# Two-layer graph attention with experts: tile 13 counted for layer 2 alone

## What is computed

```python
def _gat(x, src, dst, W, a_src, a_dst, b, heads, ch, concat):
    h = (x @ W).reshape(n, heads, ch)
    es = (h * a_src).sum(-1)
    ed = (h * a_dst).sum(-1)
    e = leaky_relu(es[src] + ed[dst], SLOPE)
    w = jnp.exp(e - segment_max(e, dst)[dst])
    alpha = w / segment_sum(w, dst)[dst]
    out = segment_sum(h[src] * alpha[:, :, None], dst)
    return (concat or mean over heads) + b

h = relu(layernorm(_gat(x, ..., 4 heads)))
x = x + _gat(h, ..., 1 head)
x = x + experts(layernorm(x))   # top 2 of 8, 256 -> 1024 -> 256, gelu
```

## Time and profile before

| what | us |
|---|---|
| median of three runs | 1459.78 |
| lowest, highest | 1451.67, 1463.59 |
| run that was profiled | 1464.53 |
| its span, first to last instruction | 1462.6 |
| PE busy | 1248.2 |
| DVE busy | 866.2 |
| ACT busy | 670.4 |
| POOL busy | 775.4 |

### The profile page before, as it was taken

One profiled execution on the slowest core, in us unless ns is written; L12 is line 12 of the kernel. 1 busy time (PEld: TensorE's weight loads), 2 busy tenths in 40 slices (PEclk: granted clock), 3 DMA queues, 4 the chain that ended last, 5 costly groups with the idle time before them and its releaser, 6 DMA issues.

```text
span 1462.6 us, 21659 instructions
## 1 busy us (share of the span) xinstructions
PE 1248.2 (85%) x6282; PEld 957.9 (65%) x6283; DVE 866.2 (59%) x2590; ACT 670.4 (46%) x1758; POOL 775.4 (53%) x682
## 2 busy tenths in 40 slices
PE   2667799989999999767798897884599999999997
PEld 1446455545555655355686676773599999999996
DVE  7679798788799877634565774766722222222221
ACT  0348676656667777532243232331033334334432
POOL 4500578676767771056666665740444445444444
PEclk9779899999999999967899998986699999999999
DMA  7002743643553481233464554433033332323221
GB/s 239 5 18 87 198 118 100 177 119 101 163 140 105 139 231 31 102 117 97 149 192 129 180 170 123 139 100 107 8 86 89 99 95 43 91 39 92 38 36 26
DMA packets 138724, 157.86 MB, mean 108 GB/s; under 512 B 60020, under 2 KB 117729, under 8 KB 138649
## 3 DMA queue, kind: packets, MB, share of 16 engines
q0 software_dynamic: 35488, 75.68, 21.1%
q1 hardware_dynamic: 101056, 79.93, 17.7%
q10 hardware_dynamic: 2104, 1.38, 0.4%
HBM read 123.00 MB, written 34.70 MB: 108 GB/s over the span
## 4 chain that ended last, share of the span: by engine, by line
PE 59%; DVE 20%; issue 9%; DMA 4%; ACT 3%; another core or an unknown queue 3%; ACTq 1%; POOL 1%; DVEq 0%; POOLq 0%; SPq 0%
PE bank L1285 12%; PE bank L1403 11%; PE bank L1411 11%; PE bank L1236 9%; PE bank L1357 7%; DVE ring_a L1896 3%; DVE ohk L1618 2%; DMA out_x<-ring_a,si 2%; PE bank L1268 2%; DVE ohs L1614 1%; PE bank L1144 1%; PE bank L1169 1%; ACT ring_a L1017 1%; DVE st L1499 1%
## 5 line engine op out<-in xcount | busy, mean ns | idle before, releaser
L772 POOL DMA_INDIRECT arena<-rows,idx_e x385 | 430.0, 1117 | 254.6 <-issue 91.8
L1285 PE MATMUL bank<-ring_a,slots 128*65 128x384 f32 (+1 forms) x1000 | 333.2, 458 | 35.9 <-DVE ring_a L1896 31.0
L1017 ACT ACTIVATE ring_a<-vbb,slots 128x384 f32<-128x384 f32 (+1 forms) x500 | 243.8, 562 | 14.7 <-DMA vbb<-v_rows 10.9
L1285 PEld LDWEIGHTS bank<-ring_a,slots 128*65 128x65 f32 x1000 | 131.4, 143 | 154.5 <-issue 99.3
L1896 DVE SCALAR_TENSOR_TENSOR ring_a<-ring_a,arena 128x1536 f32<-128x1536 f32 (+1 forms) x125 | 192.1, 1538 | 20.0 <-ACT ring_a L1017 13.4
L1114 ACT ACTIVATE ring_a<-bank,cols 128x128 f32<-128x128 f32 x432 | 128.9, 371 | 160.5 <-PE bank L1403 160.2
L1357 PE MATMUL bank<-h2t,ring_a 128*128 128x257 f32 x650 | 179.3, 416 | 24.6 <-issue 14.1
L1236 PE MATMUL bank<-arena,ring_a 128*128 128x257 f32 (+1 forms) x770 | 193.6, 400 | 5.0 <-issue 3.8
L1236 PEld LDWEIGHTS bank<-arena,ring_a 128*128 128x128 f32 x770 | 154.3, 202 | 42.6 <-issue 12.3
L1357 PEld LDWEIGHTS bank<-h2t,ring_a 128*128 128x128 f32 x650 | 129.2, 208 | 49.1 <-issue 20.7
L823 POOL DMA_INDIRECT gs<-gates,gk x54 | 51.4, 953 | 149.1 <-DVE gk L2046 143.4
(11 more groups left out here) (297 smaller groups left out, 1678.6 us busy)
## 6 DMA issues: line engine op xcount, KB each, us to landing
counts_all<-arena SPq DMA_DIRECT2D x13, 800.0 KB
arena<-counts_all SPq DMA_DIRECT2D x13, 800.0 KB
arena<-in_L_ffn_W SPq DMA_DIRECT2D x8, 1024.0 KB, 7.5
vbb<-v_pairs SPq DMA_DIRECT2D x23, 320.0 KB
arena<-rows,idx_e POOLq DMA_INDIRECT x385
XB<-general_sums SPq DMA_DIRECT2D x38, 130.0 KB
vbb<-in_L_ffn_W SPq DMA_DIRECT2D x4, 1024.0 KB
spare<-in_L_ffn_W SPq DMA_DIRECT2D x4, 1024.0 KB
```

The source lines that it names most:

```text
L772: pool.indirect_dma_start(to[:, k, 0:width], None, table, bass.IndirectOffsetOnAxis(idx_e[:, m * PAIR + k:m * PAIR + k + 1], 0)).then_inc( ...
L1017: ins = act.activation(S1[q % SLOTS1][:, h * k * P:(h + 1) * k * P].rearrange("p (t n) -> p t n", n=P), vb1[:, 0:k, h, :], ACT.Copy, scale ...
L1285: pe.matmul(bank[h][0:CH + 1, 0:w_], slots[:, s, h * (CH + 1):(h + 1) * (CH + 1)], S1[q % SLOTS1][:, h * w_:(h + 1) * w_], start=(s == 0), ...
```

## The change

Tile 13 stays an edge tile in layer 1 and becomes a dense tile in layer 2.

- `NE = 13` is now the number of dense tiles of layer 1, `ND = 14` that of layer 2. Layer 1 keeps its five blocks and 46 pairs. A sixth block of counts, `CB[5] = (13, 1)`, is made beside the steps of layer 1's last block (24 visits at steps 100 to 107) and is stored, but not used in layer 1.
- Layer 2 has seven blocks of two tiles: the last is tiles 12 and 13. Its 42 pairs (`PAIRS2`) are spread over steps 3 to 163 by `3 + p * 164 // 42`; they were 46 over steps 3 to 159. The edge tiles of layer 2 are 14 to 24. Plan steps run to 197, they ran to 191.
- SP stores the counts of tile 13 at step 126. Both first loads of layer 2's counts move to step 127, behind the waits for all stores and for the end of layer 1; the load at step 103 and the wait at step 125 are gone. POOL waits for all stores of counts before it gathers for layer 2.
- The key tables have 112 columns of windows, they had 104. `edge_row` names the row buffer of an edge tile of layer 1; its value is the one before.

The diff, cut to its core:

```diff
-ND = 13
-DW = ND * PER_TILE
-B1 = ((0, 1),) + tuple((t, min(3, ND - t)) for t in range(1, ND, 3))
+NE, ND = 13, 14
+EW, DW = NE * PER_TILE, ND * PER_TILE
+CB = ((0, 1),) + tuple((t, min(3, ND - t)) for t in range(1, ND, 3))
+B1 = CB[:1 + NE // 3]
 B2 = tuple((t, min(2, ND - t)) for t in range(0, ND, 2))
...
-PAIRS = (NW - DW) // 2
+PAIRS, PAIRS2 = (NW - EW) // 2, (NW - DW) // 2
+SKIP = PAIRS - PAIRS2
...
-for _b in range(1, len(B1)):
+for _b in range(1, len(CB)):
     for _n, (_w, _v) in enumerate(visits_of(_b)):
...
-    return min((t - ND + 1) * PER_TILE // 2, PAIRS) - 1
+    return min((t - NE + 1) * PER_TILE // 2, PAIRS) - 1
+
+
+def last_pair2(t):
+    return last_pair(t) - SKIP
...
-PAIR2 = [3 + p * 160 // PAIRS for p in range(PAIRS)]
+PAIR2 = [3 + p * 164 // PAIRS2 for p in range(PAIRS2)]
...
-    groups += [Group([t], False, PAIR2[last_pair(t)] + 2) for t in EDGE_TILES]
+    groups += [Group([t], False, PAIR2[last_pair2(t)] + 2) for t in EDGE_TILES]
...
+        def pair_of(n):
+
+            return n if n < PAIRS else n - PAIRS + SKIP
...
-                if q % NT == 1 and 0 < q // NT < len(B1):
+                if q % NT == 1 and 0 < q // NT < len(CB):
                     store_counts(q // NT)
...
-                if q == (len(B1) - 1) * NT + 3:
+                if q == Q1 + 2:
                     for par in range(2):
-                        sp.wait_ge(s_cst[par], 16 * sum(B1[b][1] for b in range(par, len(B1), 2)))
-                    sp.wait_ge(s_a, (len(B1) - 1) * NT)
+                        sp.wait_ge(s_cst[par], 16 * sum(CB[b][1] for b in range(par, len(CB), 2)))
+                    sp.wait_ge(s_a, Q1)
                     load_counts(0)
-                if q == Q1:
-                    sp.wait_ge(s_a, Q1)
                     load_counts(1)
                     sp.dma_start(fw1[0], f_w1[0].rearrange("(k p) n -> p k n", p=P)).then_inc(s_fw[0], 16)
...
             pool.memset(ring_a[:, W2_AT:W2_AT + P // PW * W_PAIR], 0.0).then_inc(s_wz, 1)
+            for par in range(2):
+                pool.wait_ge(s_cst[par], 16 * sum(CB[b][1] for b in range(par, len(CB), 2)))
             pool.wait_ge(s_ht, 16 * NT)
...
-            for n in range(PAIRS + ROW_SLOTS[1], 2 * PAIRS):
+            for n in range(PAIRS + ROW_SLOTS[1], PAIRS + PAIRS2):
                 gather_rows(n, rows2, T2W)
...
             while q < END1:
+                for w, v, u in VISITS_AT.get(q - 2, ()):
+                    if v == VISITS - 1:
+                        window_out(w)
                 for p in PAIR1_AT.get(q - 2, ()):
                     pair_out(p)
...
-                    after(act, s_on, ND + e - 1)
+                    after(act, s_on, NE + e - 1)
...
-                        act.wait_ge(s_pv, (PAIRS + last_pair(t) + 1) * PAIR)
+                        act.wait_ge(s_pv, (PAIRS + last_pair2(t) + 1) * PAIR)
```

More of the change, by code:

```diff
@@ L82 @@
 assert max(GROUP_N) <= P and DW * VISITS <= 512 and PAIR * P <= (PAD_ROWS - ROWS) * P
-assert LOOP_ROWS <= ND and (NW - DW) % 2 == 0
+assert LOOP_ROWS <= NE and (NW - EW) % 2 == 0 and B1[-1][0] + B1[-1][1] == NE
 assert MAX_TILES + NT + 1 <= SLOT_TILES
@@ L140, in plan1 @@
     groups = [Group(range(t0, t0 + k), True, NT * (b + 1)) for b, (t0, k) in enumerate(B1)]
-    for t in range(ND, NT, 2):
+    for t in range(NE, NT, 2):
         tl = range(t, min(t + 2, NT))
@@ L183, with edge_row @@
 G1, G2 = plan1(), plan2()
+def edge_row(t):
+    return 3 + (t - NE) % 2
+for _t in range(NE, NT - 2):
+    _g, _h = (next(g for g in G1 if t in g.tiles) for t in (_t, _t + 2))
+    assert _g.turn[_g.tiles.index(_t)] - 1 < _h.norm[_h.tiles.index(_t + 2)]
+for _b in range(len(B1) - 1):
+    _g, _h = (next(g for g in G1 if B1[b][0] in g.tiles) for b in (_b, _b + 1))
+    assert max(_g.turn) - 1 < min(_h.norm)
 ORDER1 = [t for g in G1 for t in g.tiles]
@@ L587, in slot_of @@
             return GL2[k], s_g[k], 16 * PAIR * (before + (n - PAIRS) // ROW_SLOTS[1] + 1)
+        def pair_of(n):
+            return n if n < PAIRS else n - PAIRS + SKIP
         def block_of(t):
-            return next(b for b, (t0, k) in enumerate(B1) if t0 <= t < t0 + k)
+            return next(b for b, (t0, k) in enumerate(CB) if t0 <= t < t0 + k)
         def tiles1(b):
-            return range(B1[b][0], B1[b][0] + B1[b][1])
+            return range(CB[b][0], CB[b][0] + CB[b][1])
         def bank_of(use):
@@ L678, in _ @@
                     else:
-                        after(sp, s_oe, t - ND - 1)
+                        after(sp, s_oe, t - NE - 1)
                         sp.dma_start(XE[:, i, 1, :], gen[t * P:(t + 1) * P, :]).then_inc(s_ge1[i], 16)
@@ L703, in _ @@
                     rows = slice(0, P if t < NT - 1 else LAST)
-                    after(sp, s_on, ND + e - 1)
+                    after(sp, s_on, NE + e - 1)
                     sp.dma_start(XB[:, e % 2, 1, :], gen[t * P:(t + 1) * P, :]).then_inc(s_gl2[e % 2], 16)
@@ L767, in gather_rows @@
                 to, s_in, _ = slot_of(n)
-                m = n % PAIRS
-                before = n - ROW_SLOTS[n // PAIRS] if m >= ROW_SLOTS[n // PAIRS] else -1
+                m = pair_of(n)
+                before = n - ROW_SLOTS[n >= PAIRS] if (n if n < PAIRS else n - PAIRS) >= ROW_SLOTS[n >= PAIRS] else -1
                 for k in range(PAIR):
@@ L869, in window_out @@
                 act.wait_ge(s_vis, (w + 1) * VISITS)
-                if b >= 2 and w == B1[b][0] * PER_TILE:
+                if b >= 2 and w == CB[b][0] * PER_TILE:
                     act.wait_ge(s_a, (b - 1) * NT)
-                    act.wait_ge(s_cst[b % 2], 16 * sum(B1[a][1] for a in range(b % 2, b - 1, 2)))
-                i, wi = t - B1[b][0], w % PER_TILE
+                    act.wait_ge(s_cst[b % 2], 16 * sum(CB[a][1] for a in range(b % 2, b - 1, 2)))
+                i, wi = t - CB[b][0], w % PER_TILE
                 act.activation(C1[b][:, :, i * P + wi * WIN:i * P + (wi + 1) * WIN],
@@ L1120, in _ @@
             pe.wait_ge(s_F, 1)
-            for g, (first, step) in enumerate(((0, 1), (DW, 2))):
+            for g, (first, step) in enumerate(((0, 1), (EW, 2))):
                 n = GROUP_N[g]
@@ L1792, in hits @@
             def hits(n, first):
-                p = n % PAIRS
+                p = pair_of(n)
                 after(v, s_pw, n)
```

30 lines of the change are left out of this document (15 added, 15 removed).

## The result

The changed kernel takes 1449.26 us (median of 20 runs, 1441.62 to 1457.54), the kernel before 1460.13 on the same chip (20 runs): ratio 0.9933, 95% interval 0.9916 to 0.9949. It is 0.7% faster, 10.9 us by the medians; the forecast was 7.3 us, or 0.5%, slower.

The account below looks back on a forecast made before the run. TensorE's work and waits were taken to set the time nearly everywhere. 7.0 - 2.3 - 14.5 + 12.9 + 4.2 = +7.3 us on 1459.8 gave 1467 us; its own range was 1458 to 1475, with rivals 1448 to 1479.

Parts of the forecast that it names:

- Layer 2, steps 0 to 149: Layer 2 before its last 25 steps: five pairs fewer at 2.7 us each and about 1.0 of finishing moved out, -14.5 us.
- Rival C: Layer 2: pairs set the pace at 7.7 us each through late slots and gathers, dense steps hidden; 1438 us, chance 0.11.
- The upper bound, 7.7 a pair: Upper case for layer 2, steps 0 to 149: the pair sets the pace, 332.0 us for 43 pairs, 38.6 us gained.
- The last 25 steps: Layer 2, steps 150 to 174: second tile 12.8 us, less 2.6 of idle time filled, plus one pair 2.7; +12.9 us.
- Costs of nothing: Before 104 us: key tables 112 windows wide instead of 104, covered by the projections; 0, uncovered under 0.3 us.
- Layer 1: Steps 99 to 107: counting tile 13's eight windows makes DVE the bound, 43.8 us instead of 37; +7.0 us.
- The one-hot row: Profile row for DVE's 400-key one-hot: 417 ns, read as about one result a nanosecond, against up to four a cycle.
- Turn: Between the layers: the small load of tile 12's sums finds SP's queue empty and takes about 2 us; -2.3 us.
- End: After the last product: a second tile adds a normalisation, 2.0 us, and transposes, copy and logits, 2.2 us; +4.2 us.
- B: Rival: one unnamed stall of 8 us moves into layer 2's longer last block; 1475 us, chance 0.18.
- D: Rival: the burst of count loads at 147 GB/s delays layer 2's first gathers by 11 us; 1478 us, chance 0.04.
- E: Rival: stalls thin out, one of 8 us goes, 1459 us; with the second tile wholly inside idle time, 1454; chance 0.20.

Follow-up runs that it names:

- b4_drop: The kernel before without tile 13 in layer 2, neither gathered nor dense: 42 pairs over steps 3 to 163, last block thin; ratio 0.9858, layer 2 339.4 us.
- b5_skip4: The kernel before with 46 pairs over steps 3 to 163, gathers of pairs 4 to 7 left out; ratio 0.9859, layer 2 352.7 us, 10.3 less than with them.
- a8_pool: The changed kernel with a sixth gather per layer-2 pair, into scratch; no ratio, layer 2 397.3 us, 59.6 us longer.
- a10_nogather: The changed kernel with the gathers of layer-2 pairs 4 to 41 left out, computation kept; ratio 0.9555, layer 2 282.5 us instead of 337.7.
- a2_close: The changed kernel with its 42 pairs as close as the 46 were, 3.48 steps each; ratio 1.0033, layer 2 16.4 us longer.
- a9_memset: The changed kernel with 1.3 us of memory fill on GpSimd per layer-2 pair; ratio 0.9955, layer 2 3.1 us longer.
- b6_tables: The kernel before with key tables 112 wide, nothing else, on the chip where the kernel before takes 1407.68 us; ratio 0.9994.
- b3_twice: The kernel before with the only product of layer 2's last block made a second time into the free bank; ratio 1.0017.
- a3_nocount: The changed kernel without counting tile 13's windows; ratio 0.9856, steps 99 to 107 of layer 1 37.2 us instead of 42.7.
- b1_turn: The kernel before with only the changed order of SP's loads between the layers; ratio 0.9984, 28.1 us between the layers.

## Why the prediction was wrong

- **Layer 2, steps 0 to 149 (-14.5, measured -29.1).** The step that failed is the price of a pair. I took 2.44 us of PE and 0.3 of waits for landings, since POOL had idle time around its gathers. Fewer pairs did make it shorter; the term left out what a gather does to others while it runs. Whole pairs are worth 5.9 us (b4_drop), their gathers alone 2.6 (b5_skip4), a sixth gather on top 1.4 (a8_pool), all of them 55 us (a10_nogather). And it added pairs to steps, as if the steps beside a pair cost their full time. They don't: from 3.48 steps a pair to 3.90, T goes from 7.43 to 7.53 us (a2_close, the changed kernel), while a step without a pair takes 1.2 us (30.9 / 25 in a2_close). The forecast had no term for the wider spacing, which gave 16.4 us. Rival C had this part right, its hidden steps. The upper bound, 7.7 a pair, was nearer, but for the reason that slots come free late and gathers pace. a9_memset and the leads of 9 to 13 us exclude that where results come late; b6_tables shows it on another chip. The forecast's own range of 1458 to 1475 didn't contain this bound: 7.7 a pair in the sum leads below 1445.
- **The last 25 steps (+12.9, measured +1.6).** The step that failed is the one that added 12.8 us of PE work and let it fill only 2.6 of 7.5 us of idle time. It filled 6.3 (7.5 before, 1.2 now), and the clock went from 0.85 to 1.00, which took the rest: PE is busy 8.0 us longer for 60 more records, where the forecast had 15.5. b3_twice shows the same for PE's part alone. The forecast worked out 3.3 us for the clock and left them out of its sum. The Trainium skill (TensorE: Matmul & The Clock Gate, "Why this matters for your kernels") says that idle gaps between bursts of matmuls bring the engine back to half rate. The trace agrees in direction: 7.5 us idle at 0.85, 1.2 us idle at 1.00.
- **Costs of nothing (0, measured +6.4).** Layer 1 started at 103.8 to 106.5 us in the five profiles with tables 104 wide and at 109.4 to 118.0 in the thirteen with 112, on chips with late results; on the one without it was 96.3 and 95.1. In the changed kernel DVE waits there for what the profile calls remote, while the 32 gathers of the tables run (waits from 28 to 60 us):

```profile
DVE es L1677 <- remote: 13.0, 2, 7.9
```

  So the width is not a cost of its own; that it moves the start through late results is argued from this, not tried alone on such a chip.
- **Layer 1 (+7.0, measured +5.4, without counting -5.5)**: right in place. DVE is busy 37.8 of 42.7 us (89%, the forecast said over 90%), and in the chain of these steps its share goes from 15.2 to 20.8 us, 5.3 of it one-hots, PE's from 9.3 to 10.1. That DVE is the bound rests on this chain: a3_nocount takes one-hots, visits and copies away together, and PE's visits are 7.1 us of records.
- **The one-hot row, misread.** The forecast read 417 ns for 400 results as one a nanosecond. Its own rows speak against it, 275 ns being the mean of blocks of 275 and of 175. Apart from GpSimd's instructions the three sizes take 317, 286 and 260 ns in the kernel before (medians): some 0.25 ns a result and over 200 ns that don't depend on the size. 47 of the 67 blocks of 400 beside a GpSimd instruction take over 450 ns, which makes the mean. So the row doesn't decide what that paragraph lets it decide; the sum took the measured means and is not touched.
- **Turn (-2.3, measured -3.1)**: in the range, but not shown for the kernel before. Its turn of 30.5 us is, with b4_drop's, the longest of the seven runs with that order, the others have 28.1 to 28.9, and b1_turn can't tell the gain from none. **End (+4.2, measured +4.1)**: right.
- **Rivals.** B and D didn't happen: no stall in the last block, and the counts behind the small load did no harm. D's sign, a first gather after 640 us, did come, at 641.4, and misleads: layer 1 ended 9.9 us later, and from its end the gather took 22.1 us, before 24.7. C's sign came too, layer 2 is 27.6 us shorter, though its reason fails where results come late; it gave 1438. E, with 1454, lies nearest, and that is luck in part: its clause of a second tile inside the idle time came true, but the stalls didn't thin out (late stretches 124 us, before 119). With the measured prices the forecast's sum would have been 7.0 - 2.3 - 5 x 5.9 + 1.6 + 4.2 = -19 us, before the start's +6.4.

What stays open: what it is in a gather that holds back PE's results, how much of the 5.9 us goes by that way, why one chip doesn't show it, and what the change brings on that chip. Idle pieces of the profile called remote or issue are where it shows; I had given them no term that grows with the number of gathers.

## What to carry to other kernels

Price a gathered piece of work by what it does to the others too, and by what lies beside it: ask whether the engine that carries the path loses idle time or clock while indirect DMAs run, and take the gathers away as an experiment, computation kept. Where work of two kinds runs side by side, vary the spacing before adding their times. Work added to a stretch in which TensorE is thin can be nearly free, since it fills gaps and keeps the clock. Before a term of nothing is written down, look whether the stretch has waits that the profile can't name.

## What the runs showed of the hardware

- While GpSimd's indirect DMAs ran, updates of TensorE's semaphores came later than the matmuls' records, by 6 us in the stretch shown, in a third of the changed kernel's layer 2 (124 of 338 us) and in 16 of 200 us of layer 1; in layer 2 after the last gather never, and on one of the chips not at all. One more gather a pair cost 59.6 us, as much time of GpSimd in fills 3.1, the same bytes by a plain DMA 5 to 13.
- The kernel before took 1461.72 to 1466.41 us on four chips and 1407.68 us on a fifth, where no result came late; layer 2 of b6_tables, which takes the same time as the kernel before there, was 318.6 us against that kernel's 365.3. A comparison holds for the chip on which it was made.
- With a product doubled in a thin block the granted clock was 1.00 instead of 0.85 (0.85 to 0.94 in the other runs with one product there), and 49 more records cost 0.7 us.
- The comparison of 400 results on DVE (16-bit tensors) took 317 ns when no GpSimd instruction overlapped it, mostly over 500 when one did; those of 175 and 275 results took 256 to 287 ns either way (medians, in the kernel before).
